# Turning the softmax sums for their reciprocals: from TensorE transposes with ScalarE copies to two 32x32 block transposes on VectorE

## The reference

```python
x = x + xattn(ctx_2048, layernorm(x), mask, mask, ...)   # 8 batches, 512 tokens, width 256
x = x + ffn(layernorm(x), ...)                           # 16 experts, top 8, and a shared one

# in xattn: 8 heads of 32
scores = einsum('bthd,bshd->bhts', q, k) / sqrt(32)      # masked
attn = softmax(scores, axis=-1)
tgt_update = einsum('bhts,bshd->bthd', attn, v)
return einsum('btf,of->bto', concat([tgt, tgt_update], axis=2), W_out) + b_out
```

## Time and profile before

| | |
|---|---|
| time, median of 3 runs | 1065.49 us (1064.21 to 1065.64) |
| span of the profiled execution, first to last instruction | 1056.2 us |
| median of the runs less that span | 9.3 us |
| TensorE busy | 1012.5 us (96%) |
| VectorE busy | 647.5 us (61%) |
| ScalarE busy | 465.9 us (44%) |
| GpSimd busy | 389.0 us (37%) |
| granted TensorE clock, mean | 0.992 |

### The profile page before, as it was taken

One profiled execution on the slowest core, in us unless ns is written; L12 is line 12 of the kernel. 1 busy time (PEld: TensorE's weight loads), 2 busy tenths in 40 slices (PEclk: granted clock), 3 DMA queues, 4 the chain that ended last, 5 costly groups with the idle time before them and its releaser, 6 DMA issues.

```text
span 1056.2 us, 14941 instructions
## 1 busy us (share of the span) xinstructions
PE 1012.5 (96%) x5198; PEld 773.3 (73%) x5198; DVE 647.5 (61%) x1469; ACT 465.9 (44%) x865; POOL 389.0 (37%) x355
## 2 busy tenths in 40 slices
PE   4789999999999998899999999999999999999998
PEld 3656767676767665567888888888888888888886
DVE  5877777877777557355565555555555555555544
ACT  3346565656665646545323323333333333332322
POOL 3379797879797967345210010010010100100000
PEclk9899999999999999999999999999999999999999
DMA  7343433434333223324222121121220230221220
GB/s 239 104 131 78 131 81 111 108 84 131 73 110 75 65 65 105 92 86 131 75 80 61 52 80 50 61 81 40 72 80 31 71 90 20 91 80 31 93 68 20
DMA packets 65674, 87.87 MB, mean 83 GB/s; under 512 B 10720, under 2 KB 31088, under 8 KB 65600
## 3 DMA queue, kind: packets, MB, share of 16 engines
q1 hardware_dynamic: 63680, 84.83, 28.0%
q10 hardware_dynamic: 1920, 2.10, 0.6%
HBM read 56.97 MB, written 4.46 MB: 58 GB/s over the span
## 4 chain that ended last, share of the span: by engine, by line
PE 91%; DVE 4%; ACT 2%; SPq 1%; issue 1%; DMA 1%; POOL 0%; DVEq 0%; ACTq 0%
PE ps L653 50%; PE pst L653 18%; PE ps L732 6%; PE ps L759 5%; PE pst L748 5%; PE ps L659 4%; PE ps L772 1%; DVE mx L1201 1%; ACT e_buf L868 1%; SPq L606 1%; PE ps L811 1%; SPq L541 1%; ACT ctx_h L868 0%; DVE wsrc_l L1148 0%; PE ps L812 0%
## 5 line engine op out<-in xcount | busy, mean ns | idle before, releaser
L653 PE MATMUL ps<-x_h,weights 128*128 128x512 f32 x1088 | 365.6, 397 | 1.4 <-DVE x L1194 0.8
L653 PEld LDWEIGHTS ps<-x_h,weights 128*128 128x128 f32 x1088 | 204.5, 188 | 51.8 <-issue 1.0
L1201 DVE TENSOR_REDUCE mx<-ps 128x1 f32<-128x512 f32 x256 | 173.3, 685 | 81.8 <-PE ps L732 80.9
L868 ACT ACTIVATE hh<-qb 128x512 fp32r<-128x512 f32 x136 | 86.0, 632 | 296.4 <-DVE qb L1315 273.7
L653 PE MATMUL ps<-x_l,weights 128*128 128x512 f32 x544 | 214.6, 395 | 0.0
L653 PE MATMUL pst<-hh,weights 128*128 128x512 f32 x544 | 194.6, 399 | 0.0
L1304 DVE TENSOR_TENSOR qb<-ps,sg 128x512 f32<-128x512 f32 x136 | 94.1, 692 | 160.2 <-PE ps L653 153.8
L868 ACT ACTIVATE e_buf<-pst 128x512 f32<-128x512 f32 x256 | 147.4, 596 | 92.8 <-PE pst L748 81.8
L1317 DVE TENSOR_TENSOR hl<-qb,hh 128x512 fp32r<-128x512 f32 x136 | 94.3, 693 | 95.0 <-ACT hh L868 95.0
L1407 POOL TENSOR_TENSOR e_sums<-e_sums,e_buf 128x1024 f32<-128x1024 f32 x60 | 143.5, 2391 | 7.2 <-ACT e_buf L868 1.2
L1359 POOL TENSOR_SCALAR ve<-mv 128x4 f32<-128x4 f32 x8 | 1.8, 226 | 347.1 <-DVE mv L1242 347.1
(11 more groups left out here) (159 smaller groups left out, 1391.5 us busy)
## 6 DMA issues: line engine op xcount, KB each, us to landing
cb<-combine_scratch SPq DMA_DIRECT2D x128, 256.0 KB, 3.2
q_stack<-q_h SPq DMA_DIRECT2D x128, 64.0 KB, 2.0
k_stack<-k_h SPq DMA_DIRECT2D x124, 64.0 KB, 2.0
ctx_raw<-in_ctxT SPq DMA_DIRECT2D x7, 1024.0 KB, 5.2
q_stack<-q_l SPq DMA_DIRECT2D x64, 64.0 KB, 2.0
out_x<-ob SPq DMA_DIRECT2D x16, 256.0 KB, 2.2
k_stack<-k_l SPq DMA_DIRECT2D x62, 64.0 KB, 2.0
x<-in_x SPq DMA_DIRECT2D x7, 512.0 KB, 6.5
```

The lines of the kernel that those rows point to most:

```text
L653: ins = engine.matmul(dst, lhsT, rhs, start=start and n == 0, stop=stop and n == len(terms) - 1)
L868: return engine.activation(dst, src, func, **kw)
L1201: engine.tensor_reduce(MX[:, g % 2, h // 2, h % 2, q:q + 1], bank(step), AX.X, ALU.max).then_inc(sem("max"), 1)
```

## The change

The sums are no longer turned by TensorE. Where head `i` has its sum for token `32c + r` on partitions `32i` to `32i + 31` in column `32c + r`, a transpose of each 32x32 block puts it on partition `32i + r`, in each column of block `c`. One column of every 32 is taken to its reciprocal, and a second block transpose, that reads each reciprocal 32 times, puts it back. Both are done by VectorE, the first straight from PSUM. The output `OP` is no longer copied: `norm_u` reads it in PSUM.

```diff
-        at(t + 19.8, ("out_o", g))
-        at(t + 22.2, ("turn_s", g))
-        at(t + 21.2, ("recip", g))
-        at(t + 22.3, ("spread", g))
-        at(t + 25.4, ("turn_r", g))
-        at(t + 25.3, ("norm_u", g))
-        at(t + 26, ("hi_u", g))
+        at(t + 21.9, ("sums_t", g))
+        at(t + 22.4, ("recip", g))
+        at(t + 22.9, ("spread", g))
+        at(t + 23.9, ("norm_u", g))
+        at(t + 24.6, ("hi_u", g))
...
-         if s[0] in ("q", "y", "shift", "turn_x", "turn_s", "turn_r", "turn_x2", "turn_c", "bo")
+         if s[0] in ("q", "y", "shift", "turn_x", "turn_x2", "turn_c", "bo")
...
-        RU = s1("ru", [128, 4, 4, 1])
+        RU = s1("ru", [128, S // HD, 1])
...
             if kind == "attend":
-                return sem("s_sb"), s[1] + 1
-            if kind == "turn_s":
-                return sem("recip"), s[1] + 1
-            if kind == "turn_r":
-                return sem("u_norm"), s[1] + 1
+                return sem("sums_t"), s[1] + 1
...
                     if part == 0 and g > 0:
-                        pe.wait_ge(sem("o_sb"), g)
+                        pe.wait_ge(sem("u_norm"), g)
...
-                elif kind == "turn_s":
...
-                elif kind == "turn_r":
...
-                elif kind == "out_o":
...
-                elif kind == "spread":
...
+                elif kind == "sums_t":
+                    g = step[1]
+                    dve.wait_ge(*burst_done(g, 1))
+                    if g > 0:
+                        dve.wait_ge(sem("u_norm"), g)
+                    engine.transpose(SS[:, :], bank(sums_step(g))).then_inc(sem("sums_t"), 1)
                 elif kind == "recip":
                     g = step[1]
-                    dve.wait_ge(sem("s_turned"), g + 1)
+                    dve.wait_ge(sem("sums_t"), g + 1)
                     if g > 0:
                         dve.wait_ge(sem("spread"), g)
-                    engine.reciprocal(RU[:, :, :, :], bank(("turn_s", g)).rearrange("p (q h d) -> p q h d", q=4, h=4)[:, :, :, 0:1]
-                                      ).then_inc(sem("recip"), 1)
+                    engine.reciprocal(RU[:, :, :], SS[:, :].rearrange("p (c r) -> p c r", r=HD)[:, :, 0:1]).then_inc(
+                        sem("recip"), 1)
+                elif kind == "spread":
+                    g = step[1]
+                    dve.wait_ge(sem("recip"), g + 1)
+                    engine.transpose(SS[:, :].rearrange("p (c r) -> p c r", r=HD),
+                                     RU[:, :, :].to_broadcast([128, S // HD, HD])).then_inc(sem("spread"), 1)
                 elif kind == "norm_u":
                     g = step[1]
-                    dve.wait_ge(sem("r_turned"), g + 1)
-                    dve.wait_ge(sem("o_sb"), g + 1)
-                    engine.tensor_tensor(OS[:, :], bank(("turn_r", g)), OS[:, :], ALU.mult).then_inc(sem("u_norm"), 1)
+                    dve.wait_ge(sem("spread"), g + 1)
+                    if g > 0:
+                        dve.wait_ge(sem("ut_lo"), g)
+                    engine.tensor_tensor(OS[:, :], OP[:, :], SS[:, :], ALU.mult).then_inc(sem("u_norm"), 1)
```

More of the change, by code:

```diff
@@ L822, in tensor_program @@
                     pe.wait_ge(sem("u_norm"), NG)
-                    pe.wait_ge(sem("o_sb"), NG)
                     pe.wait_ge(sem("exp"), 2 * NU)
```

## The result

| | before | after |
|---|---|---|
| median of 4 runs | 1064.85 us (1063.19 to 1065.64) | 1072.13 us (1069.35 to 1073.99) |
| ratio | | 1.0077 (95%: 1.0051 to 1.0102) |
| profiled execution: span / its own time | 1056.2 us / none given | 1071.8 us / 1073.99 us |

The forecast was 1059.0 us, within 1050.5 to 1064.5. By the medians the change costs 7.3 us (0.7%; the ratio on record is 1.0077), where 6.5 us less were forecast. Two executions that ran at a far lower clock than all others, one of the kernel before (1668 us at 0.558) and one of e15 (1259 us at 0.747), stand in no ratio here.

A forecast was written before the change was run, and what follows sets the result against it. TensorE was taken to bound the first stage. Savings of 12.74 + 1.03 + 0.5 = 14.3 us, less 7.8 us given back in waits, leave 6.5 us: 1065.5 - 6.5 = 1059.0 us, range 1050.5 to 1064.5.

The forecast's parts named there:

- The transposes: Two 128x512 transposes added per group on VectorE, priced at 0.65 and 0.68 us from a plain copy out of PSUM.
- Slow transposes: Rival: each VectorE transpose takes 1.56 us, like the mask row, giving 1080.6 us; chance 0.1.
- I take 0.65, a little under the sum: TensorE's new wait for late row maxima, 0.65 us in each of 12 groups, 7.8 us given back.
- The working itself: Following VectorE's queue up to the awaited maximum: TensorE waits 0.74 us in a first group, 0.7 in a second.
- The break-even of a steady group: The wait per group beyond which the change loses: 1.2 us, reached at about 0.95 us per transpose.
- the maxima swallow it: Rival: TensorE waits 1.0 to 1.2 us per group for row maxima, giving 1063.2 to 1065.6 us; chance 0.1.
- the gains outside the steady groups: Savings counted for all the stage, 14.3 us, while new waits were charged to only 12 groups.
- 1.5 us on ScalarE and GpSimd: Savings from two copies on the chain, 1.03 us, and the last group's earlier low part of `u`, 0.5 us.
- which has 9.3 us around it: The difference between the profiled span of 1056.2 us and the median of 1065.49 us, carried over unchanged.
- the far end of the prediction's price for a transpose: Upper end for a VectorE transpose, from the slow 512-element mask row: median 1556 ns.

The follow-up runs named there:

- e15: The changed kernel with `norm_u` and `hi_u` back at their old, later due times in groups 0 to 11 only: 1067.23 us, ratio 1.0031.
- e17: e13 with the second transpose written into the sums' PSUM bank, so `norm_u` has one operand in PSUM: 1073.63 us, ratio 1.0086.
- e3: The kernel before, with two more VectorE operations per group that nobody waits for, at the transposes' due times: 1062.53 us, ratio 1.0003.
- e16: The changed kernel with `norm_u` and `hi_u` back at their old, later due times in groups 12 to 15 only: 1068.22 us, ratio 1.0040.
- e2: The changed kernel with both VectorE transposes cut to one 32x32 block, leaving out the other 15 blocks' reciprocals: 1064.68 us, ratio 1.0002.
- e1: The changed kernel with `norm_u` and `hi_u` back at their old, later due times in all groups: 1060.45 us, ratio 0.9970.
- e13: The changed kernel at its own due times, with ScalarE copying `OP` out of PSUM again and `norm_u` reading that copy: 1109.95 us, ratio 1.0455.
- e10: The changed kernel with ScalarE's copy of `OP`, `norm_u` at its old due time, three banks for maxima and two for the ring: 1057.55 us, ratio 0.9935.
- e5: The changed kernel without any transposes, VectorE taking the reciprocal of the whole 128x512 tile from PSUM: 1107.52 us, ratio 1.0403.

## Why the prediction was wrong

**What held.** The transposes: 0.65 and 0.68 us forecast, 0.706 and 0.712 measured; 0.71 had been the estimate from the Trainium skill, "VectorE: DVE Perf Modes", "The three transpose paths", and the trace agrees. Slow transposes are out. `recip` and `norm_u` cost what they cost before. `attend` doesn't wait for `norm_u` (e17; 0.4 us once in the waits of after). And the place was right: the waits grew just ahead of `attend` part 0, by the fourth maximum, behind `norm_u`.

**The step that failed first: "I take 0.65, a little under the sum".** The working itself gave 0.74 us of wait in a first group and 0.7 in a second; after has 1.05 and 0.83. Rounding down had no row behind it, and which tenths of VectorE's queue make up the other 0.31 and 0.13 us was not followed. The term also lacked the 0.2 us that TensorE's first matmul after an idle time takes longer. A wait of 0.94 and a restart of 0.2 give 1.1 us in place of 0.65. Over 12 groups this is 12 x 0.47 = 5.6 us (6.7 us with the 1.21 of a whole batch) of the 13.8 us between the forecast and what the change did (7.3 + 6.5). A batch is 0.66 us longer, not 0.5 shorter, with VectorE busy for 38.53 of its 50.11 us, 77% and not 82%. The break-even of a steady group is its 0.88 us of turns, only 0.14 us above the working; the prediction put it at 1.2 us, by setting the gains of the whole stage against the waits of these 12 groups. The rival "the maxima swallow it" had a wait of 1.0 to 1.2 us, which is what came, and a chance of 0.1 only.

**The second: the gains outside the steady groups were kept whole.** The sum counted 12 groups with a wait and took the turns of the rest (and 1.5 us on ScalarE and GpSimd) as won, at a clock of 1.00 everywhere. In group 5 and in the last four groups the waits for maxima are longest, 1.45 and 3.73 us (e3 has 2.30 for the latter), and the clock is at its lower level behind them; in the last groups it is low in e15, e16 and e17 too, in group 5 it need not be (e17). Against the profiled execution of e3 (1062.62 us, near the median of before) that of after (1073.99) loses 6.4 us up to group 12, 4.0 of them in group 5 (2.7 against the profile of before, as the gate row of e3 is short), and 4.1 us from there to the last `attend`. No step of the prediction had a price for waits outside the steady groups or for a lower clock. How the loss there divides between the two is not shown.

**The third: "which has 9.3 us around it".** In the later runs the time is 2.2 to 2.3 us more than the span (1.8 to 1.9 in e2). So the profiled execution of before, 1056.2 us, took about 1058.4 us: it was 7 us faster than the median and faster than each of 82 others, with a clock of 0.992 where those have 0.986 in the mean. For the sum this did no harm, as a difference was added to the median. But it hid what the second step needed. In that trace the clock from 420 to 470 us is 1.00; in e3, nearly the same kernel in an ordinary execution, it is 0.94 there, and 16 matmuls of `attend` take 3.5 us instead of 1.85. By the mean clocks the stage lost more of its clock in most executions than in the trace that I read. There is no trace of an ordinary execution of before that would show where.

**Where the loss comes from, in one sentence:** it needs the turns gone (TensorE 0.88 us earlier), the transposes on VectorE (e2 without most of them: no loss), and `norm_u` ahead of the maxima (e1 without that: a gain of 0.3%); the same load beside the turns costs nothing in the steady groups (e3).

## What to carry to other kernels

When work moves from the engine that bounds a stage to one that works in bursts, price it by what stands behind it in that engine's queue at the moment when the first engine asks, and take as the margin the old slack less the time that the first engine has won; the busy share says nothing of it. Then look at the order before giving up the change: one step, 0.7 us long, moved behind the maxima that TensorE waits for was worth 11 us, more than the change itself. And set the profiled execution's own time against the median first: a trace 0.7% faster than the median may have a clock that most executions don't get.

## What the runs showed of the hardware

- A product on VectorE with both operands in SBUF takes 0.69 us alone and 2.4 us (median) beside an SBUF operation of GpSimd of 2.4 us (e13); with one operand in PSUM it takes 0.68 in the same order (e17). In e10 its median is 0.69 us but its longest 2.71, so the best version still pays for it. The Trainium skill, "SBUF — State Buffer", "Who interferes with whom", says that a VectorE instruction with two SBUF inputs contends with a GpSimd instruction that reads SBUF; these runs agree.
- Two operations of VectorE with a single tensor operand in SBUF are held up in the same way. The gate row takes 2.50 us where it starts 0.02 us after a GpSimd operation of some 2.4 us, and 0.33 us in e3, where it starts 0.08 us ahead of one:

```profile
197.30 2.50 DVE L1210 TENSOR_SCALAR gate_sb<-gate_sb,gate_r 16x256 f32<-16x256 f32 x1
197.28 4.89 POOL L1388 TENSOR_TENSOR e_sums<-e_sums,e_buf 128x1024 f32<-128x1024 f32 x2
```

  The mask row, which I had taken as slow by its form, takes 0.42 us at 18.59 with GpSimd idle, and 2.17 us at 56.30, beside a GpSimd operation that ends at 58.18, 0.29 us before it does. So the far end of the prediction's price for a transpose was no price of an operation's form.
- A block transpose takes time by its columns: 0.206 us for 32 and 0.706 for 512 out of PSUM. Out of SBUF, with each element read 32 times, it takes 0.712 us, nearly the same.
- A reciprocal is dear per column, 6.3 ns (e5), where other operations with 512 columns take 0.66 to 0.69 us in all.
- TensorE's first `max` matmul after an idle time takes 0.47 us to the next start, where it takes 0.24 in a row. Where its clock is at the lower level, the six matmuls at 204.90 take 2.56 us instead of 1.38. TensorE's busy time is then no measure of its work: it has 128 instructions fewer and is busy for 0.5 us more.
